# Storing only two of the three bf16 parts of q and k ahead of the loads for the row maxima

## The chip, the cores and the metric

The kernel runs on one core of a Trainium2 chip. The metric is the device time of one execution in microseconds (us), lower is better. The engines are TensorE (PE, its weight loads PEld), VectorE (DVE), ScalarE (ACT), GpSimd (POOL) and SyncE (SP), which here issues all DMAs.

## The reference

The input x has 16 images of 256 tokens and 128 channels. Four layers are added to it one after the other: x = x + layer(layernorm(x)). The first is a state-space layer with 32 heads. The second is a transformer block, the third mixes shifted tokens through gates, and the fourth is the same transformer block again. Only the attention inside the transformer block (it runs twice for each image, as "layer 0" and "layer 1" of the kernel) is touched:

```python
def _attention(src, Wq, bq, Wk, bk, Wv, bv, Wo, bo):
    q = (src @ Wq + bq).reshape(B, T, NHEAD, HEAD_DIM)      # 16 heads of 8
    k = (src @ Wk + bk).reshape(B, T, NHEAD, HEAD_DIM)
    v = (src @ Wv + bv).reshape(B, T, NHEAD, HEAD_DIM)
    scores = jnp.einsum('bqhd,bkhd->bhqk', q, k) * scale
    probs = jax.nn.softmax(scores, axis=-1)
    out = jnp.einsum('bhqk,bkhd->bqhd', probs, v).reshape(B, T, d)
    return out @ Wo + bo
```

It is followed by `x1 = ln(src + attn_out)`, a mixture of 8 experts and `ln(x1 + ff)`.

## The kernel before

The work is written as a list of "hops" (`PERIOD`), each with a name, a layer, a step and a lag. One pass over the list is a turn. In turn t a hop with lag l works on image t - l, so a turn holds pieces of up to six images, and there are 16 turns with a new image and some at either end in which the list is only partly filled (turns are counted from 0 here). Every engine walks through the same list in the same order and does its own part of each hop; semaphores connect the parts. An engine that waits in one hop delays all its later hops, so the order of the list is the schedule.

The score matrix is computed with bf16 operands. q and k (128 rows, one per head and channel, by 256 tokens) are each split into three bf16 parts that add up to the f32 value. The hop `q` does this, with step 1 for k and step 0 for q:

- PE multiplies (L746), ACT writes the f32 value `qkf` (L1034) and the first part (L1035).
- POOL subtracts the first part (L1494), casts the rest to the second part (L1496) and subtracts again for the third part (L1498), which raises `split_done`. Behind k's parts it also adds `b_o` to `src` (L1502) and `ln2_b` to `x` (L1503), for later hops.
- SP waits for `split_done` and stores the parts to DRAM in the layout in which they will be read: for q the first two parts, twice (L541); for k all three parts, three times (L545, L547).

The hop `mload` follows. SP waits until the stores of k and then of q have landed and loads both for the maxima (`k_max`, `q_max`, L556, four DMAs a side; only rows made of the first two parts are read). Behind them it stores what is left of q: the first two parts once more (L559) and the third part three times (L562). The hop `sload` loads all 72 rows (`k_stack`, `q_stack`, L571).

The hop `smax` multiplies `q_max` with `k_max` on PE (L765), and DVE takes the maxima (`rowmax`, L1295). They become one more row of `q_stack` (`maxt`), and the hops `es`, `exps` and `ep` do the scores, exponentials and the product with v.

In the list k comes first in layer 0 and q comes first in layer 1. The list around the changed hops:

```
layer 0: q0.1 down0.4 ... q0.0 ... experts0.2 ... mix1.0 ... tail1.3 ... mload0.0 tap0.6 xcopy0.2
         xcopy0.4 tap0.7 mix1.1 taps0.6 place0.0 tail1.4 taps0.7 mix1.2 bcp0.0 mix1.3 ... smax0.0
layer 1: q1.0 es0.1 exps0.1 own0.5 sum0.2 q1.1 up1.4 ... mload1.0 ... own0.6 ... sload1.0 ... smax1.0
```

Other work of POOL near these hops: the reciprocal roots of the layer norms (L1437 and L1439, for `experts0.2`, `mix1.0` and `tail1.3`), the addition of `mix_b` to x (`mix1.2`, L1513), `bc_prod` (`bcp0.0`, L1451), the sums of the mixing layer (L1519) and the products `own` (L1529). Other work of DVE there: the convolution taps (L1220, one input in PSUM, one in SBUF), the edge correction of the convolution (L1230, both inputs in SBUF, 6 columns), the normalisation of `mix1.1` (L1114), the last step of a layer norm (`tail1.4`, L1127, two instructions, both inputs in SBUF), the mixing products (L1408) and the decay products `att` (L1247).

Of the kernel before, what the change touches and what calls it, by code (L numbers as in the profile page):

```python
# [11 lines left out]
P = 128  # L12
BATCH, T, HID = 16, 256, 128
NT = T // P
# [181 lines left out]
def build(nc, d, out):  # L196
# [12 lines left out]
    with ctx:  # L209
# [3 lines left out]
        def sem(name):  # L213
            return ctx.enter_context(nc.semaphore(name))
# [155 lines left out]
        src_ready, split_done, nmax_ready = sem("src_ready"), [sem("q_split"), sem("k_split")], sem("nmax_ready")  # L370
        x1_ready, gate_in, gate_exp, we_ready = sem("x1_ready"), sem("gate_in"), sem("gate_exp"), sem("we_ready")
# [31 lines left out]
        for hop in hops:  # L403
            if (hop[0], hop[3]) in (("q", 1), ("mix", 2)):
                offsets[hop[:3]] = len(offsets) + 1

        bo_adds = {}
        for hop in hops:
            if (hop[0], hop[3]) == ("q", 1):
                bo_adds[hop[1], hop[2]] = len(bo_adds) + 1  # L410
# [90 lines left out]
        def _(e):  # L501
# [11 lines left out]
            for hop in hops:  # L513
# [20 lines left out]
                elif what == "q":  # L534
# [4 lines left out]
                    if k == 0:  # L539
                        for copy in range(2):  # L540
                            e.dma_start(dram(qk_scrd[0], 2 * copy * P * T, [[T, P], [P * T, 2], [1, T]]),  # L541
                                        qparts_b[0][:, 0:2, :]).then_inc(qk_stored[0], 16)
                    else:
                        for copy in range(2):
                            e.dma_start(dram(qk_scrd[1], copy * P * T, [[T, P], [2 * P * T, 3], [1, T]]),  # L545
                                        qparts_b[1][:, :, :]).then_inc(qk_stored[1], 16)
                        e.dma_start(dram(qk_scrd[1], 6 * P * T, [[T, P], [P * T, 3], [1, T]]),  # L547
                                    qparts_b[1][:, :, :]).then_inc(qk_stored[1], 16)
                elif what == "mload":
# [3 lines left out]
                    for side in (1, 0):  # L553
                        e.wait_ge(qk_stored[side], (96 * u + 32, 48 * (u + 1))[side])
                        for g in range(RG):
                            e.dma_start((q_max, k_max)[side][32 * g:32 * g + MAXROWS, :, :].rearrange("r s t -> r (s t)"),  # L556
                                        dram(qk_scrd[side], g * HPG * T, [[NH * T, MAXROWS], [1, HPG * T]])).then_inc(
                                            max_loaded[side], 16)
                    e.dma_start(dram(qk_scrd[0], 4 * P * T, [[T, P], [P * T, 2], [1, T]]),  # L559
                                qparts_b[0][:, 0:2, :]).then_inc(qk_stored[0], 16)  # L560
                    for copy in range(3):
                        e.dma_start(dram(qk_scrd[0], (6 + copy) * P * T, [[T, P], [1, T]]),  # L562
                                    qparts_b[0][:, 2, :]).then_inc(qk_stored[0], 16)
                elif what == "sload":
# [4 lines left out]
                    for side in (1, 0):  # L569
                        e.wait_ge(qk_stored[side], (96, 48)[side] * (u + 1))  # L570
# [335 lines left out]
        def _(e):  # L906
# [6 lines left out]
            for hop in hops:  # L913
# [114 lines left out]
                elif what == "q":  # L1028
                    t, b, u = bank(hop)
                    if nth[hop]:  # L1030
                        e.wait_ge(split_done[k], nth[hop])
                        e.wait_ge(qk_stored[k], (96, 48)[k] * nth[hop])
# [69 lines left out]
        def _(e):  # L1102
# [44 lines left out]
            for hop in hops:  # L1147
# [239 lines left out]
                elif what == "experts" and k == 3:  # L1387
                    ff, s = ff_b[lay], ln_slot(what, lay)
                    e.wait_ge(rstd_ready, roots["experts", lay, n, 2])
                    e.wait_ge(x_offset, offsets["q", lay, n])  # L1390
# [34 lines left out]
        def _(e):  # L1425
# [4 lines left out]
            for hop in hops:  # L1430
# [59 lines left out]
                elif what == "q":  # L1490
# [5 lines left out]
                    e.tensor_copy(qparts[:, 1, :], qr).then_inc(*own.step())  # L1496
                    e.wait_ge(*own.now())
                    e.tensor_tensor(qparts[:, 2, :], qr, qparts[:, 1, :], ALU.subtract).then_inc(split_done[k], 1)  # L1498
                    if k == 1:
                        e.wait_ge(rest_loaded, 16 * len(rest_consts))  # L1500
                        e.wait_ge(*full(("fn", lay, n, 1)))
                        e.tensor_tensor(src_b[lay][:, :, :], src_b[lay][:, :, :], bc(b_o[:, :], 1, NT), ALU.add).then_inc(src_bo, 1)  # L1502
                        e.tensor_tensor(xb[:, :, :], xb[:, :, :], bc(ln2_b[:, :], 1, NT), ALU.add).then_inc(x_offset, 1)  # L1503
# [78 lines left out]
```

## Time and profile before

| | |
|---|---|
| time, median of 3 runs | 2107.03 us (2103.94 to 2107.87) |
| the profiled execution | 2103.15 us, its span 2101.4 us |
| busy: PE, DVE, ACT, POOL | 91%, 83%, 71%, 37% of the span |
| mean granted TensorE clock | 0.966 of full speed |
| distance of two full turns | 119.4 us (the same DVE instruction at 1065.28 and at 1184.66 us) |

The span is the time from the first to the last instruction; 1.75 us of the execution lie outside it. In a full turn PE and DVE are busy almost all the time. At either end of the execution the list is only partly filled, and there the engines wait for single steps of the attention.

### The profile page before, as it was taken

To read this page: it belongs to the slowest core of one execution; us is meant where nothing else is said; L and a number is where in the kernel's file an instruction comes from. 1 tells how busy PE (TensorE), PEld (TensorE's weight loads), DVE (VectorE), ACT (ScalarE), POOL (GpSimd) and SP (SyncE) were. 2 spreads that over 40 slices of the span, in tenths; PEclk is the share of its full clock that TensorE was granted. 3 is DMA by queue.
4 is the path that set the end of the run, shared out by engine and by line. 5 is a ranking of instruction groups with operands and counts; after the bars stand their busy time and mean duration, and the time that the engine had idled before them with its cause. 6 is when DMAs were issued, how large, how long until landed. Compare 5 with 4: busy or idle time off the path is not lost.

```text
span 2101.4 us, 48245 instructions
## 1 busy us (share of the span) xinstructions
PE 1921.0 (91%) x16928; PEld 1491.0 (71%) x16928; DVE 1738.5 (83%) x4463; ACT 1488.0 (71%) x3207; POOL 775.6 (37%) x1139
## 2 busy tenths in 40 slices
PE   4779899999999999999999999999999999997757
PEld 3556677777877777786877778786777778774545
DVE  5776988989898988989898998989898898865643
ACT  4566768778686868778686877868686877855332
POOL 5313353525243343525244352424334352423120
PEclk8889999999999999999999999999999999998867
DMA  5021232211222222211222222121222221112110
GB/s 162 12 63 12 60 67 60 65 41 46 50 59 67 62 67 63 56 35 51 59 60 67 62 64 56 45 44 54 67 60 67 62 63 38 50 53 71 27 56 6
DMA packets 224576, 117.14 MB, mean 56 GB/s; under 512 B 124360, under 2 KB 210512, under 8 KB 219216
## 3 DMA queue, kind: packets, MB, share of 16 engines
q1 hardware_dynamic: 224336, 114.06, 21.5%
q8 instruction: 137, 2.24, 0.5%
q14 instruction: 103, 0.84, 0.1%
HBM read 67.60 MB, written 46.14 MB: 54 GB/s over the span
## 4 chain that ended last, share of the span: by engine, by line
PE 64%; DVE 23%; ACT 4%; issue 4%; SPq 2%; POOL 2%; DMA 1%; DVEq 0%; ACTq 0%; POOLq 0%
DVE nmax L1295 6%; PE psA L862 6%; PE psB L724 6%; DVE work L1220 5%; PE psB L874 5%; PE psA L874 5%; PE psA L699 5%; PE psB L803 3%; PE psB L862 3%; PE psA L630 3%; PE psB L699 2%; PE psA L803 2%; DVE att L1247 2%; DVE hid L1408 2%; PE psA L788 2%
## 5 line engine op out<-in xcount | busy, mean ns | idle before, releaser
L1247 DVE TENSOR_TENSOR att<-att,QK 128x1024 f32<-128x1024 f32 x192 | 251.2, 1341 | 15.2 <-ACT att L1003 15.1
L1529 POOL TENSOR_TENSOR own<-X,ccoef 128x512 f32<-128x512 f32 x128 | 160.2, 1257 | 206.7 <-PE psA L699 97.1
L1437 POOL TENSOR_SCALAR var_eps<-lnmv 128x2 f32<-128x2 f32 x128 | 40.4, 316 | 524.0 <-DVE lnmv L1110 521.3
L1220 DVE SCALAR_TENSOR_TENSOR work<-psA,c_conv_w,work 128x255 f32<-128x255 f32 (+2 forms) x450 | 195.4, 474 | 11.8 <-ACT work L961 11.8
L630 PE MATMUL psA<-xnT_a,c_w_in 128*128 128x256 f32 x608 | 177.9, 397 | 17.8 <-DVE hid L1220 8.7
L1072 ACT ACTIVATE hid<-psA,c_b 128x256 f32<-128x256 f32 x295 | 135.8, 485 | 79.4 <-PE psA L862 79.2
L1295 DVE TENSOR_REDUCE nmax<-psB 128x2 f32<-128x512 f32 x288 | 186.6, 680 | 1.1 <-PE psB L765 1.1
L862 PE MATMUL psA<-x1T,c_w 128*128 128x256 f32 x608 | 178.9, 394 | 1.5 <-DVE nmax L1295 1.3
L1049 ACT ACTIVATE pt<-psB 128x512 f32<-128x512 f32 x256 | 147.4, 614 | 31.5 <-PE psB L789 31.4
L1295 DVE TENSOR_REDUCE nmax<-psA 128x2 f32<-128x512 f32 x224 | 149.8, 681 | 15.1 <-PE psA L765 14.9
L1220 DVE SCALAR_TENSOR_TENSOR work<-psB,c_conv_w,work 128x255 f32<-128x255 f32 (+1 forms) x360 | 159.0, 474 | 2.7 <-ACT work L961 2.1
L874 PE MATMUL psB<-c_w,hid 128*128 128x128 f32 x1152 | 160.6, 285 | 0.4 <-ACT hid L1072 0.4
L874 PEld LDWEIGHTS psB<-c_w,hid 128*128 128x128 f32 x1152 | 148.3, 199 | 8.8 <-issue 4.2
L1519 POOL TENSOR_TENSOR O_sb<-O_sb,hid 128x256 f32<-128x256 f32 x128 | 98.8, 772 | 148.8 <-DVE hid L1408 141.6
L1049 ACT ACTIVATE pt<-psA 128x512 f32<-128x512 f32 x256 | 150.3, 618 | 0.1
L1379 DVE SCALAR_TENSOR_TENSOR ff<-psB,w_e,ff 128x128 f32<-128x128 f32 x288 | 86.8, 342 | 73.1 <-PE psB L874 71.4
L630 PE MATMUL psB<-xnT_a,c_w_in 128*128 128x256 f32 x480 | 137.9, 392 | 0.8 <-ACT hid L1072 0.7
L862 PE MATMUL psB<-x1T,c_w 128*128 128x256 f32 x416 | 125.3, 396 | 13.0 <-DVE nmax L1295 11.9
L630 PEld LDWEIGHTS psA<-xnT_a,c_w_in 128*128 128x128 f32 x608 | 107.3, 196 | 39.6 <-DVE hid L1220 10.3
L1003 ACT ACTIVATE att<-psA 128x512 f32<-128x512 f32 x176 | 96.6, 599 | 53.4 <-PE psA L670 51.9
L1003 ACT ACTIVATE att<-psB 128x512 f32<-128x512 f32 x208 | 114.9, 603 | 21.6 <-PE psB L670 18.8
L724 PE MATMUL psB<-c_w_out,Z 128*128 128x128 f32 x1024 | 124.3, 280 | 3.8 <-DVE c_w_out L1260 3.8
(326 smaller groups left out, 5375.3 us busy)
## 6 DMA issues: line engine op xcount, KB each, us to landing
qk_scr<-kparts SPq DMA_DIRECT2D x96, 192.0 KB, 2.4
k_stack<-qk_scr SPq DMA_DIRECT2D x32, 576.0 KB
q_stack<-qk_scr SPq DMA_DIRECT2D x32, 576.0 KB
qk_scr<-qparts SPq DMA_DIRECT2D x96, 128.0 KB, 1.9
k_max<-qk_scr SPq DMA_DIRECT2D x128, 64.0 KB, 2.0
q_max<-qk_scr SPq DMA_DIRECT2D x128, 64.0 KB, 2.0
lvl_scr<-work SPq DMA_DIRECT2D x32, 192.0 KB, 5.7
qk_scr<-qparts SPq DMA_DIRECT2D x96, 64.0 KB, 1.7
```

Of the source, the lines that this page charges most:

```text
L630: e.matmul(t[:, 0:T], w_in[:, first + j * P:first + (j + 1) * P], xnT_a[:, :], start=True, stop=True).then_inc(filled[b], 1)
L699: m = e.matmul(t[j * HD:(j + 1) * HD, f * P:(f + 1) * P], X[:, s, fc + j * HD:fc + (j + 1) * HD], att[:, 2 * f + j, :], start=False, stop= ...
L724: m = e.matmul(t[:, k * P:(k + 1) * P], Z[:, f, k * P:(k + 1) * P], w_out[:, f, :], start=(f == 0), stop=(f == NF - 1))
L862: e.matmul(t[:, 0:T], w_1[:, k, j * P:(j + 1) * P], x1T_b[lay][:, :], start=True, stop=True).then_inc(filled[b], 1)
L874: m = e.matmul(t[:, i * P:(i + 1) * P], hb[:, j, i * P:(i + 1) * P], w_2[:, 2 * k + j, :], start=(j == 0), stop=(j == 1))
L1003: e.activation(att[:, :, c:c + 64], t[:, :].rearrange("p (t h) -> p h t", h=HG), ACT.Exp).then_inc(drained[b], 1)
L1049: e.activation(pt_b[a % PTS][:, :, :].rearrange("p h q -> p (h q)"), t[:, :], ACT.Exp, scale=float(AD) ** -0.5).then_inc(drained[b], 1)
L1072: e.activation(hid_b[lay][k % 2][:, j, :], t[:, 0:T], ACT.Relu, bias=b_1[:, 2 * k + j:2 * k + j + 1]).then_inc(drained[b], 1)
L1220: m = e.scalar_tensor_tensor(out=cv[:, back:], in0=t[:, 0:T - back], scalar=conv_w[:, c, tap:tap + 1], in1=cv[:, back:], op0=ALU.mult, op1 ...
L1247: e.tensor_tensor(att[:, :, :], att[:, :, :], bc(QK[:, kq, :], 1, HG), ALU.mult).then_inc(att_done, 1)
L1295: e.tensor_reduce(nmax[:, i, p0:p0 + 2], t[:, :].rearrange("p (h k) -> p h k", k=T), AX.X, ALU.max).then_inc(drained[b], 1)
L1529: e.tensor_tensor(own_b[k % 2][:, :].rearrange("p (h c) -> p h c", c=HD), X[:, tt, h0 * HD:(h0 + HG) * HD].rearrange("p (h c) -> p h c", c ...
```

## The change

In hop `q` POOL makes only the second part and raises `split_done` behind it. SP stores only the first two parts, twice, for k as for q. The third parts move into hop `mload` on POOL: k's, then q's, each raising a new semaphore `third_done`, and behind them the two additions of `b_o` and `ln2_b`. In hop `mload` SP loads the side that was stored first first (layer 0 k, layer 1 q). Behind the loads it waits for k's third part, stores the rest of k in two DMAs and the first two parts of q once more, waits for q's third part and stores it three times with one DMA. DVE's later wait for `x_offset` is counted from the hop `mload`.

```diff
@@ SP, hop q
-                    if k == 0:
-                        for copy in range(2):
-                            e.dma_start(dram(qk_scrd[0], 2 * copy * P * T, [[T, P], [P * T, 2], [1, T]]),
-                                        qparts_b[0][:, 0:2, :]).then_inc(qk_stored[0], 16)
-                    else:
-                        for copy in range(2):
-                            e.dma_start(dram(qk_scrd[1], copy * P * T, [[T, P], [2 * P * T, 3], [1, T]]),
-                                        qparts_b[1][:, :, :]).then_inc(qk_stored[1], 16)
-                        e.dma_start(dram(qk_scrd[1], 6 * P * T, [[T, P], [P * T, 3], [1, T]]),
-                                    qparts_b[1][:, :, :]).then_inc(qk_stored[1], 16)
+                    for copy in range(2):
+                        first, step = ((2 * copy, 1), (copy, 2))[k]
+                        e.dma_start(dram(qk_scrd[k], first * P * T, [[T, P], [step * P * T, 2], [1, T]]),
+                                    qparts_b[k][:, 0:2, :]).then_inc(qk_stored[k], 16)
@@ SP, hop mload
-                    for side in (1, 0):
-                        e.wait_ge(qk_stored[side], (96 * u + 32, 48 * (u + 1))[side])
+                    for side in ((1, 0), (0, 1))[lay]:
+                        e.wait_ge(qk_stored[side], 64 * u + 32)
...
+                    e.wait_ge(third_done[1], u + 1)
+                    e.dma_start(dram(qk_scrd[1], 4 * P * T, [[T, P], [P * T, 2], [1, T]]),
+                                bc(qparts_b[1][:, 2, :], 1, 2)).then_inc(qk_stored[1], 16)
+                    e.dma_start(dram(qk_scrd[1], 6 * P * T, [[T, P], [P * T, 3], [1, T]]),
+                                qparts_b[1][:, :, :]).then_inc(qk_stored[1], 16)
                     e.dma_start(dram(qk_scrd[0], 4 * P * T, [[T, P], [P * T, 2], [1, T]]),
                                 qparts_b[0][:, 0:2, :]).then_inc(qk_stored[0], 16)
-                    for copy in range(3):
-                        e.dma_start(dram(qk_scrd[0], (6 + copy) * P * T, [[T, P], [1, T]]),
-                                    qparts_b[0][:, 2, :]).then_inc(qk_stored[0], 16)
+                    e.wait_ge(third_done[0], u + 1)
+                    e.dma_start(dram(qk_scrd[0], 6 * P * T, [[T, P], [P * T, 3], [1, T]]),
+                                bc(qparts_b[0][:, 2, :], 1, 3)).then_inc(qk_stored[0], 16)
@@ POOL, hop q, then hop mload
-                    e.tensor_copy(qparts[:, 1, :], qr).then_inc(*own.step())
-                    e.wait_ge(*own.now())
-                    e.tensor_tensor(qparts[:, 2, :], qr, qparts[:, 1, :], ALU.subtract).then_inc(split_done[k], 1)
-                    if k == 1:
-                        e.wait_ge(rest_loaded, 16 * len(rest_consts))
-                        e.wait_ge(*full(("fn", lay, n, 1)))
-                        e.tensor_tensor(src_b[lay][:, :, :], src_b[lay][:, :, :], bc(b_o[:, :], 1, NT), ALU.add).then_inc(src_bo, 1)
-                        e.tensor_tensor(xb[:, :, :], xb[:, :, :], bc(ln2_b[:, :], 1, NT), ALU.add).then_inc(x_offset, 1)
+                    e.tensor_copy(qparts[:, 1, :], qr).then_inc(split_done[k], 1)
+                elif what == "mload":
+                    for k in (1, 0):
+                        qr, qparts = qkf[:, k, :], qparts_b[k]
+                        e.wait_ge(split_done[k], nth[hop] + 1)
+                        e.tensor_tensor(qparts[:, 2, :], qr, qparts[:, 1, :], ALU.subtract).then_inc(third_done[k], 1)
+                    e.wait_ge(rest_loaded, 16 * len(rest_consts))
+                    e.wait_ge(*full(("fn", lay, n, 1)))
+                    e.tensor_tensor(src_b[lay][:, :, :], src_b[lay][:, :, :], bc(b_o[:, :], 1, NT), ALU.add).then_inc(src_bo, 1)
+                    e.tensor_tensor(xb[:, :, :], xb[:, :, :], bc(ln2_b[:, :], 1, NT), ALU.add).then_inc(x_offset, 1)
```

ACT's hop `q` now waits for `third_done` and for 64 instead of 96 and 48 counts of `qk_stored`, and `sload` waits for 64.

## Rows read from the trace of the kernel before

**Rows 1.** The page: busy time, share of the span and instructions of each engine

```profile
PE 1921.0 (91%) x16928; PEld 1491.0 (71%) x16928; DVE 1738.5 (83%) x4463; ACT 1488.0 (71%) x3207; POOL 775.6 (37%) x1139
```

**Rows 2.** Waits over the whole span: us in total, times, longest us

```profile
PEld psA L765 <- DMA q_max<-qk_scr: 14.5, 3, 9.4
```

**Rows 3.** Timeline, first image, layer 0: start us, us, engine, line, operation

```profile
132.15 0.48 ACT L1035 ACTIVATE qparts<-psA,c_bq 128x256 bf16<-128x256 f32 x1
...
133.61 0.67 POOL L1494 TENSOR_TENSOR qkf<-qkf,qparts 128x256 f32<-128x256 f32 x1
...
135.52 0.88 SPq L541 DMA_DIRECT2D qk_scr<-qparts  x2
...
143.81 0.28 PE L765 MATMUL psA<-k_max,q_max 32*128 32x256 bf16 x1 [3.13 <-DMA q_max<-qk_scr]
```

**Rows 4.** Timeline, last image but one, layer 1

```profile
1942.86 0.28 PE L765 MATMUL psA<-k_max,q_max 32*128 32x256 bf16 x1 [1.49 <-DMA q_max<-qk_scr]
```

**Rows 5.** Chain of work that ended last, last image, layer 1

```profile
2022.91 0.67 POOL qparts L1498
...
2024.76 0.68 POOL kparts L1498
...
2026.39 2.54 DMA qk_scr<-kparts
...
2032.14 1.97 DMA q_max<-qk_scr
```

**Rows 6.** Timeline, last image, layer 1

```profile
2028.99 1.71 SPq L556 DMA_DIRECT2D k_max<-qk_scr  x4
...
2034.15 0.39 PE L765 MATMUL psA<-k_max,q_max 32*128 32x256 bf16 x1 [9.00 <-DMA q_max<-qk_scr]
```

**Rows 7.** Timeline of POOL, a full turn, layer 0

```profile
1175.08 0.67 POOL L1498 TENSOR_TENSOR kparts<-qkf,kparts 128x256 bf16<-128x256 f32 x1
1175.72 0.72 POOL L1502 TENSOR_TENSOR src<-src,c_bo 128x256 f32<-128x256 f32 x1
1176.41 0.72 POOL L1503 TENSOR_TENSOR x<-x,c_ln_b 128x256 f32<-128x256 f32 x1
...
1185.30 0.73 POOL L1513 TENSOR_TENSOR x<-x,c_beta 128x256 f32<-128x256 f32 x1
```

**Rows 8.** Timeline of VectorE, the same turn

```profile
1187.26 0.17 DVE L1230 TENSOR_TENSOR work<-work,conv_edge 128x6 f32<-128x6 f32 x1
1187.37 0.61 DVE L1127 SCALAR_TENSOR_TENSOR x<-x,lnrs,c_ln_b 128x128 f32<-128x128 f32 x2
```

**Rows 9.** Chain of work that ended last, the same turn

```profile
1187.37 0.61 DVE x L1127 x2
```

**Rows 10.** Line 1127, from 1894.3 to 1896.5 us: ns min/median/max, first and last start

```profile
L1127 DVE SCALAR_TENSOR_TENSOR x<-x,lnrs,c_ln_b x2: 339/628/917, 1894.7 to 1895.5; 128x128 f32<-128x128 f32 x2
```

**Rows 11.** Timeline of POOL at that place

```profile
1894.70 0.72 POOL L1513 TENSOR_TENSOR x<-x,c_beta 128x256 f32<-128x256 f32 x1
```

**Rows 12.** Timeline of POOL and VectorE, layer 1 of a full turn

```profile
1115.50 1.34 POOL L1502 TENSOR_TENSOR src<-src,c_bo 128x256 f32<-128x256 f32 x1
...
1116.29 0.63 DVE L1194 TENSOR_TENSOR work<-SPL,c_neg_a 128x64 f32<-128x64 f32 x1
...
1117.49 1.49 POOL L1529 TENSOR_TENSOR own<-X,ccoef 128x512 f32<-128x512 f32 x1
...
1120.90 3.22 DVE L1247 TENSOR_TENSOR att<-att,QK 128x1024 f32<-128x1024 f32 x2
```

**Rows 13.** Timeline of VectorE, the turn in which a tap ended late

```profile
1423.91 2.50 DVE L1220 SCALAR_TENSOR_TENSOR work<-psB,c_conv_w,work 128x255 f32<-128x255 f32 x6
1426.87 0.17 DVE L1230 TENSOR_TENSOR work<-work,conv_edge 128x6 f32<-128x6 f32 x1 [0.46 <-DVE work L1220]
...
1543.60 2.49 DVE L1220 SCALAR_TENSOR_TENSOR work<-psB,c_conv_w,work 128x255 f32<-128x255 f32 x6
```

**Rows 14.** Timeline of VectorE, first image in the mixing layer

```profile
235.43 0.61 DVE L1114 SCALAR_TENSOR_TENSOR src<-x,lnmv,lnrs 128x128 f32<-128x128 f32 x2 [1.21 <-POOL lnrs L1439]
```

More of the change, by code:

```diff
@@ L370, in build @@
         src_ready, split_done, nmax_ready = sem("src_ready"), [sem("q_split"), sem("k_split")], sem("nmax_ready")
+        third_done = [sem("q_third"), sem("k_third")]
         x1_ready, gate_in, gate_exp, we_ready = sem("x1_ready"), sem("gate_in"), sem("gate_exp"), sem("we_ready")
@@ L403, in build @@
         for hop in hops:
-            if (hop[0], hop[3]) in (("q", 1), ("mix", 2)):
+            if (hop[0], hop[3]) in (("mload", 0), ("mix", 2)):
                 offsets[hop[:3]] = len(offsets) + 1
@@ L408, in build @@
         for hop in hops:
-            if (hop[0], hop[3]) == ("q", 1):
+            if hop[0] == "mload":
                 bo_adds[hop[1], hop[2]] = len(bo_adds) + 1
@@ L569, in _ @@
                     for side in (1, 0):
-                        e.wait_ge(qk_stored[side], (96, 48)[side] * (u + 1))
+                        e.wait_ge(qk_stored[side], 64 * (u + 1))
                         e.dma_start((q_stack, k_stack)[side][0:ROW_MAX, :, :].rearrange("r s t -> r (s t)"),
@@ L1030, in _ @@
                     if nth[hop]:
-                        e.wait_ge(split_done[k], nth[hop])
-                        e.wait_ge(qk_stored[k], (96, 48)[k] * nth[hop])
+                        e.wait_ge(third_done[k], nth[hop])
+                        e.wait_ge(qk_stored[k], 64 * nth[hop])
                     e.wait_ge(filled[b], u + 1)
@@ L1389, in _ @@
                     e.wait_ge(rstd_ready, roots["experts", lay, n, 2])
-                    e.wait_ge(x_offset, offsets["q", lay, n])
+                    e.wait_ge(x_offset, offsets["mload", lay, n])
                     e.wait_ge(*own.now())
```

## Prediction

> **What bounds the kernel.** I read the page first [rows 1]: TensorE is busy 91% of the span and VectorE 83%, and in a full turn both are near their limit. So a step of the attention's preparation costs time only where one of them stands still for it. The list of waits shows where that is [rows 2]: over 32 attentions TensorE waits for the maxima's loads only three times, 14.5 us in all on the weight-load side, 9.4 of them once. In all other attentions the loads have long landed and earlier hops of the list set the start of `smax`. The timelines give the three places: the first image in layer 0 [rows 3], the last image but one in layer 1 [rows 4] and the last image in layer 1 [rows 5, 6]. On TensorE's own side these waits are 3.13, 1.49 and 9.00 us. The chain of work passes through them, POOL's split, the store, its landing, the loads [rows 5].
>
> In the full turns I then looked for what POOL's work touches, because that work is moved. The chain of work goes there through VectorE, instruction after instruction, and one of its pieces is `tail1.4`, L1127 [rows 8, 9].
>
> **What the change gives, place by place.**
>
> First image, layer 0. ACT's first part of q is there at 132.63, but POOL begins q's remainder only at 133.61, since k's third part and the two additions are ahead of it [rows 3]. Without these it could begin up to 0.98 us earlier; I take 0.84, with a little for the hand-over from ACT. q's own third part, 0.67 us (the duration in [rows 5, 7]), leaves the way of the stores too. The stores, the loads and their landing follow in the same order, so `smax` comes 1.5 us earlier than 143.81. TensorE's wait of 3.13 us leaves room for it. **-1.5 us.**
>
> Last image but one, layer 1. The loads gain one third part, 0.67 us, and the landing of k's third store; the order q before k also lets q's loads run while k's stores land. That is over 3 us by the sum of the next paragraph, but TensorE waits only 1.49 [rows 4]. **-1.5 us.**
>
> Last image, layer 1. k's remainder can start where q's third part starts now, 2022.91, and k's parts are ready after a subtraction and a cast, at 2024.1, where now they end at 2025.44 [rows 5]. Now the third store leaves at 2026.39 and takes 2.54 us to land, and the eight loads run from 2028.99 on, k's four in 1.71 us and q's four in about as long again, the last of them issued at 2032.14 [rows 5, 6]. After the change the two k stores leave at 2024.1 and 2024.5 and land by 2027.05 at the same 2.54. q's stores left at 2022.9 and 2023.3, so q's loads run from 2025.3 to 2027.1 in that shadow. k's run from 2027.1 to 2028.9, the last is issued at 2028.5 and lands 1.97 us later [rows 5]. TensorE starts at 2030.5 instead of 2034.15. **-3.6 us.** Its wait shrinks from 9.00 to about 5.4, so all of it is taken out of the wait.
>
> Together -6.6 us. All other stores and loads have slack. Issues fall from nine to eight an attention at the same bytes; SP's new waits for the third parts stand behind the maxima's loads, and what is queued behind them, `lvl` and `sload`, is needed by hops many microseconds later. I cost both at nothing. If that slack were gone, a late third part would delay `es`, and TensorE with it.
>
> **What the move on POOL costs.** In layer 0 of a full turn the third parts and the additions leave a place where POOL was otherwise idle: k's third part and both additions run from 1175.08 to 1177.13 there, all at their shortest durations [rows 7], beside taps that read one input from PSUM. They go to the hop `mload`, just ahead of `mix1.2`, which now begins at 1185.30 [rows 7]. By the spacings of [rows 7] (0.64, then 0.69) the four take 0.64 + 0.64 + 0.69 + 0.69 = 2.66 us: k's third from 1185.30, q's from 1185.94, `b_o` 1186.58 to 1187.30, `ln2_b` 1187.27 to 1187.99, and then `mix1.2` and `bcp0.0` behind them without a gap until about 1189.4. POOL was idle there from 1186.7 on. Now VectorE has L1230 at 1187.26 and the pair L1127 from 1187.37 to 1187.98 [rows 8].
>
> Such a pair does not run beside a POOL instruction. At 1894.65 an instruction of L1127 takes 917 ns and the other 339 [rows 10]; POOL's addition runs from 1894.70 to 1895.42 [rows 11], and the long one ends 0.15 us after it. So it waited for POOL's end although it had started first. In layer 1 L1194, 64 columns, takes 0.63 us and ends 0.08 after POOL's addition; that addition took 1.34 instead of 0.72, so POOL waits as well [rows 7, 12]. The Trainium skill, "SBUF — State Buffer", section "Who interferes with whom", has the rule: a VectorE instruction with two SBUF inputs and a GpSimd instruction that reads SBUF exclude each other, and whoever issues first keeps the port for the whole instruction. The trace agrees on the exclusion and not on the order, since the 917 ns instruction had the earlier start; applied to the order of starts worked out here, the rule would give the same result as the rows.
>
> Worked through: L1230 slips in at 1187.30 between two additions, as L1194 did. The first L1127 waits for the end of `ln2_b` at 1187.99 and ends at 1188.14. `mix1.2` had to wait, runs the 0.60 us that a blocked addition takes after its release (1.34 - 0.74 in [rows 12]), and ends at 1188.74. The second L1127 ends 0.15 later, 1188.89, against 1187.98 now: **+0.91 us**. It's a piece of the chain [rows 9], and the taps behind it follow at once, so the turn grows by it. How much comes through is shown once: at 1426.87 L1230 started 0.36 us late [rows 13], and that turn lasted 119.69 us (1423.91 to 1543.60) where its neighbours last 119.39, 0.30 more. I take 0.06 off: +0.85 us. The bounds per turn: 0.57 if only one POOL instruction is met (917 - 346), 1.5 if L1230 misses its gap and each of three instructions waits. I take the value of the exact alignment.
>
> It repeats in the turns that have `taps0.6`, `tail1.4` and `mload0.0`: 13 of them, turns 4 to 16, in all of which the present timeline is the same within 0.1 us. **13 x 0.85 = +11.0 us.** In turn 3 the same place holds L1114, whose pair starts 0.03 us before POOL is free for k's third part [rows 14]: **+0.9 us** by the same reckoning, between 0 and 1.2.
>
> Layer 1 of a full turn: q's third part leaves a place where it only ran ahead of a wait of POOL for TensorE, and comes behind k's. `own` at 1117.49 [rows 12] starts some 1.1 us later, alone (about 1.04 us), and ends near 1119.7, before the two `att` at 1120.90. Cost 0. Without that margin of 1.2 us the cost would be up to 0.8 in each of 16 turns, which is what one `own` adds to the pair of `att` today (3.22 against 2 x 1.21).
>
> **Sum.** -6.6 + 11.0 + 0.9 = +5.3 us. The profiled execution, 2103.15, becomes 2108.4. It lies 3.9 us under the median of the runs; the difference is carried over, so the median 2107.03 becomes **2112.3 us**.
>
> **Rivals.**
> 1. *The exclusion costs nothing*, because POOL's block falls between VectorE's two-input instructions or the slip is made up in the turn. For it: the moved work took nothing from VectorE in its old place, and POOL has 63% idle. Against it: the block is 4 us without a gap around a fixed chain of VectorE. Then the three places at the ends are all: 2107.03 - 6.6 = 2100.4, faster. It decides from where less than 0.5 us of collisions a turn is left (6.6 over 14 turns).
> 2. *Half of it*: one collision a turn, 0.5 us, 13 times, +0.5 in turn 3: -6.6 + 7.0 = +0.4, 2107.4, no difference.
> 3. *Every collision at its worst*: 14 x 1.45 - 6.6 = +13.7, 2120.7. It decides from L1230 missing its gap, a matter of 0.1 us.
> 4. *The change doesn't do what it says*: the ends keep their waits because the store of k lands later in two parts than in three. Nothing in [rows 5] speaks for it; with the collisions it gives 2107.03 + 11.9 = 2118.9.
>
> **Chances.** The forecast (collisions of 0.85 to 1.1 a turn, 2111 to 2116 with the scatter of the runs) 0.48, rival 3 0.07, rival 4 0.05, rival 2 0.25, rival 1 0.15. The measurement can tell about 0.2%, 4.2 us, from no change. Faster by more 0.15; within it 0.25; slower 0.60. The range leaves out rival 1 and a little of rival 3: 2104 to 2120. The forecast's own range is 2109 to 2117.
>
> **What the new profile would show.** The waits for the maxima's loads: 3.13 becomes about 1.6, 1.49 goes, 9.00 becomes about 5.4. SP's third k store is gone ahead of `mload`. In turns 4 to 16 L1127 of `tail1.4` has a duration near 0.8 to 1.0 us instead of 0.35, POOL is busy from the third parts to `bc_prod` without a gap, and two full turns are 120.2 us apart instead of 119.4. If L1127 stays at 0.35, or the turns stay at 119.4, the prediction is wrong and the kernel is faster. If L1230 takes 0.8 too, the time is nearer to 2120. If `att` grows in layer 1, I placed `own` wrongly.

## The result and the profile after

The changed kernel takes 2127.09 us, the median of 4 runs (2124.05 to 2128.53), beside 2105.49 us for the kernel before on the same chip (2103.29 to 2107.87). The ratio is 1.0099, with a 95% interval of 1.0087 to 1.0112: slower by 21.6 us. I predicted 2112.3 us, between 2104 and 2120. The sign was right, but the forecast change was +5.3 us where +21.6 was measured, and the time lies outside the range.

The profiled execution took 2128.53 us with a span of 2126.7. The profiled one of before took 2103.15, so the two traces differ by 25.4 us, 4 us more than the medians.

The page of the changed kernel, where [rows 1] stood, shows TensorE with the same instructions and 17 us more of busy time:

```profile
PE 1938.3 (91%) x16928; PEld 1503.5 (71%) x16928; DVE 1754.9 (83%) x4463; ACT 1494.4 (70%) x3207; POOL 768.6 (36%) x1139
```

Its list of waits over the whole span, two rows:

```profile
PEld psA L834 <- issue: 20.9, 15, 3.6
...
PE psA L834 <- DVE x L1127: 18.4, 14, 3.4
```

The same two rows before:

```profile
PEld psA L834 <- issue: 3.6, 1, 3.6
PE psA L834 <- DVE x L1127: 3.4, 1, 3.4
```

L834 is TensorE's transpose of the `x` that L1127 writes. The one wait of 3.4 us, in the last image, was there before; the 13 of the full turns are new. Timelines of a full turn in layer 0, POOL, then VectorE, then TensorE. They answer to [rows 7, 8], one turn earlier:

```profile
1079.46 0.67 POOL L1501 TENSOR_TENSOR kparts<-qkf,kparts 128x256 bf16<-128x256 f32 x1
...
1081.41 0.72 POOL L1505 TENSOR_TENSOR x<-x,c_ln_b 128x256 f32<-128x256 f32 x1
1082.09 0.72 POOL L1515 TENSOR_TENSOR x<-x,c_beta 128x256 f32<-128x256 f32 x1
1082.77 0.77 POOL L1451 TENSOR_TENSOR bc_prod<-work 128x256 f32<-128x256 f32 x1
```

```profile
1081.42 0.73 DVE L1230 TENSOR_TENSOR work<-work,conv_edge 128x6 f32<-128x6 f32 x1
1082.07 1.62 DVE L1127 SCALAR_TENSOR_TENSOR x<-x,lnrs,c_ln_b 128x128 f32<-128x128 f32 x2
```

```profile
1083.84 0.30 PE L834 MATMUL psA<-c_ident,x 128*128 128x128 f32 x1 [1.17 <-DVE x L1127]
```

Read the ends. L1230 starts at 1081.42, 0.01 us behind the start of the addition of `ln2_b`, and ends at 1082.15, 0.02 behind its end. The first L1127 starts at 1082.07 and ends behind `mix1.2` (1082.81); the second ends at 1083.69, behind `bc_prod` (1083.54). So each of VectorE's three instructions waits out one POOL instruction. POOL's own keep 0.72 us, and only `bc_prod` has 0.05 more. Matched one by one with those of the trace before, the three add 0.57, 0.52 and 0.47 us of delay: 1.55 together. The two L1127 do this in all 13 full turns; L1230 takes 0.73 to 0.75 us in 11 of them and 0.25 and 0.38 in the other two (turns 12 and 13).

That is not all of it. The turns are not equally long. ScalarE's `maxT`, one of its two in each of three turns in a row (timeline of ScalarE, changed kernel; the other one of each turn is left out):

```profile
499.43 0.36 ACT L1041 ACTIVATE maxT<-psA 16x256 bf16<-16x256 bf16 x1
...
621.89 0.36 ACT L1041 ACTIVATE maxT<-psA 16x256 bf16<-16x256 bf16 x1
...
742.74 0.36 ACT L1041 ACTIVATE maxT<-psA 16x256 bf16<-16x256 bf16 x1
```

One turn lasts 122.46 us and the next 120.85, where 119.39 was the rule before. The table by stretches, for two stretches of about the same length that begin with L834, one in a long and one in a short turn (columns: us, then the busy time of TensorE, its weight loads, VectorE, ScalarE and POOL, the granted clock, DMA share, GB/s), and TensorE's timeline in the long one:

```profile
596.10:600.20 4.10, 4.10 (x13) 3.34 (x14) 3.74 (x10) 1.77 (x5) 0.73 (x1) 0.58 0.72 187
1083.80:1088.00 4.20, 4.17 (x32) 3.76 (x32) 3.98 (x10) 2.38 (x7) 0.73 (x1) 1.00 0.69 191
```

```profile
596.10 0.30 PE L834 MATMUL psA<-c_ident,x 128*128 128x128 f32 x1 [1.18 <-DVE x L1127]
...
597.16 1.06 PE L893 MATMUL psA<-srcT,c_w_mix 128*128 128x256 f32 x2
```

In 4.1 us TensorE starts 13 matmuls of the long turn, and in 4.2 us 32 of the short one. Behind the wait for L1127 the granted clock is 0.58 in the mean, most of the stretch at 1.2 GHz. Two matmuls of L893 take 1.06 us where they take 0.59 at the full clock. In the trace of before the clock is never low between 300 and 1890 us; in that of the changed kernel it is low in eight places in that time. Each begins at L834, between 0.7 us ahead of its start, inside the wait, and 0.3 us behind it.

The wait of [rows 4] is gone. The other two ends of the execution, timelines of TensorE in the first image and, with SP, in the last, which answer to [rows 3, 6]:

```profile
144.22 0.28 PE L765 MATMUL psA<-k_max,q_max 32*128 32x256 bf16 x1 [2.34 <-DMA q_max<-qk_scr]
```

```profile
2059.48 0.37 PE L765 MATMUL psA<-k_max,q_max 32*128 32x256 bf16 x1 [5.43 <-issue]
```

```profile
2054.20 1.71 SPq L551 DMA_DIRECT2D q_max<-qk_scr  x4
2055.96 1.81 SPq L551 DMA_DIRECT2D k_max<-qk_scr  x4
```

In the last image k's loads now come last, so it fits that TensorE's wait there no longer carries the name of q's.

The account of the two traces, from `maxT` of each attention in both (the changed kernel's start less that of before). Up to the third attention it is 0.6 us late; the traces of the experiments lie there between 3.7 us early and 1.7 late. The 13 turns 4 to 16 cost 1.46 us each, 19.0. The eight half clocks cost 12.4, in seven of those turns seen as 1.2 to 2.8 us more than 1.46. Two odd losses of before, 1.3 us near 432 and 0.3 at [rows 13], are not there any more: -1.6. The turn behind them adds 0.6. The last image but one gives back 1.55 and the last 4.07. Together 0.6 + 19.0 + 12.4 - 1.6 + 0.6 - 1.55 - 4.07 = 25.4 us.

The odd loss near 432 is a late landing, TensorE's timeline before:

```profile
429.72 0.27 PE L788 MATMUL psB<-q_stack,k_stack 96*128 96x256 bf16 x1 [1.19 <-DMA q_stack<-maxT]
```

Waits of 0.7 to 1.2 us for this load are in single turns of some of the traces below, here or at other places, and in none of the changed kernel's full turns. They are scatter between executions, up to about 1.3 us each.

### The profile page after: what moved, and what is told of

Its sections match the earlier page's. It is cut to its first block, busy times and chain, and to the rows that moved or that the text cites. A ratio compares the mean times of both kernels' runs of the same rounds, so it can differ in the third digit from the quotient of the medians.

```text
span 2126.7 us, 48213 instructions
## 1 busy us (share of the span) xinstructions
PE 1938.3 (91%) x16928; PEld 1503.5 (71%) x16928; DVE 1754.9 (83%) x4463; ACT 1494.4 (70%) x3207; POOL 768.6 (36%) x1139
## 4 chain that ended last, share of the span: by engine, by line
PE 66%; DVE 21%; ACT 4%; issue 4%; SPq 2%; POOL 1%; DMA 1%; DVEq 0%; ACTq 0%; POOLq 0%
DVE nmax L1295 6%; PE psA L862 6%; PE psB L724 6%; PE psB L874 5%; PE psA L874 5%; PE psA L699 5%; DVE work L1220 4%; PE psB L862 3%; PE psB L803 3%; PE psA L630 3%; PE psB L699 3%; PE psA L803 2%; PE psA L788 2%; DVE att L1247 2%; PE psB L630 2%
## 5 line engine op out<-in xcount | busy, mean ns | idle before, releaser
L1531 POOL TENSOR_TENSOR own<-X,ccoef 128x512 f32<-128x512 f32 x128 | 154.1, 1209 | 212.8 <-PE psA L699 112.3
L1003 ACT ACTIVATE att<-psB 128x512 f32<-128x512 f32 x208 | 114.9, 603 | 21.6 <-PE psB L670 18.8
```

What stands on the lines that cost most here:

```text
L1003: e.activation(att[:, :, c:c + 64], t[:, :].rearrange("p (t h) -> p h t", h=HG), ACT.Exp).then_inc(drained[b], 1)
L1531: e.tensor_tensor(own_b[k % 2][:, :].rearrange("p (h c) -> p h c", c=HD), X[:, tt, h0 * HD:(h0 + HG) * HD].rearrange("p (h c) -> p h c", c ...
```

## The experiments

Three ideas were tested: that POOL's block costs by colliding with VectorE, that TensorE's wait costs a second time through its clock, and against both, that SP's later stores and new waits cost. Ratios are to the kernel before, run beside them on the same chip.

**e1_layer0_back.** Layer 0's POOL work out of `mload`, to the end of hop `q`:

```diff
-                elif what == "mload":
+                if (what, lay, k) == ("q", 0, 0) or (what, lay) == ("mload", 1):
                     for k in (1, 0):
...
```

The counts of `x_offset` and `src_bo` follow. What was expected:

> The changed kernel, with layer 0's third parts and its two additions taken out of the hop mload again and put behind q's split, at the end of the hop q; the stores, the loads and all of layer 1 stay as changed. My theory: all that the full turns lost (two full turns 120.9 to 122.4 us apart instead of 119.4) comes from POOL's block meeting VectorE's L1230 and L1127. Then the full turns are back at 119.4 us, L1230 and L1127 at 0.17 and 0.35 us, TensorE is granted the full clock through all full turns, and only the gains at the ends are left: 1.5 and 4 us in the last two images and 0.8 in the first, so some 6 us under the kernel before, about 2100 us. Rival: SP's side costs the time (k's third stores behind the maxima's loads, the later landing of the last store, the new waits in SP's queue): then the full turns stay longer and the time stays near 2120 to 2127 us.

Measured: 2122.26 us, ratio 1.0076 (1.0064 to 1.0089). Neither theory had this. L1230 and L1127 are short again, as I expected, but the turns last 120.8 us. The timeline of VectorE, then that of POOL, show why:

```profile
1189.37 1.35 DVE L1122 SCALAR_TENSOR_TENSOR ff<-ff,lnmv,c_ln_g 128x128 f32<-128x128 f32 x2
...
1192.33 0.61 DVE L1127 SCALAR_TENSOR_TENSOR x<-ff,lnrs,x 128x128 f32<-128x128 f32 x2 [0.88 <-POOL lnrs L1439]
```

```profile
1190.53 0.78 POOL L1505 TENSOR_TENSOR x<-x,c_ln_b 128x256 f32<-128x256 f32 x1
1191.28 0.22 POOL L1437 TENSOR_SCALAR var_eps<-lnmv 128x2 f32<-128x2 f32 x1
```

The block now stands ahead of a root of the experts' norm. The pair L1122, 0.61 us before, waits out two POOL instructions, and POOL comes to the root at 1191.28, so VectorE then waits 0.88 for it. That is 1.4 us a turn by another route. TensorE waits 0.37 us ahead of L834 in most of these turns, and one of them has a half clock. The expectation failed in taking q's end for empty: in the kernel before, q's third part ends just ahead of that pair. One place was replaced by another bad one; the SP theory is tested by e8 below.

**e2_adds_back.** Only the two additions back into `q`, behind k's split; the third parts stay in `mload`:

```diff
+                if what == "mload":
                     for k in (1, 0):
...
+                if (what, lay, k) == ("q", 0, 1) or (what, lay) == ("mload", 1):
                     e.wait_ge(rest_loaded, 16 * len(rest_consts))
...
```

> The changed kernel, with only layer 0's two additions (b_o, ln2_b) put back into the hop q of side k; the two third parts stay in mload. POOL's block ahead of mix1.2 is then 2 instructions (1.28 us) longer than before instead of 4 (2.66 us). Theory that each of VectorE's three instructions (L1230, L1127 twice) waits for the end of the POOL instruction under way and POOL for none of them: bc_prod now runs from about 1187.3 to 1188.0 by the times of the kernel before, so L1230 waits 0.55 us and the pair after it finds POOL idle: +0.5 to 0.6 us a turn, 7 us over 13 turns, less 6 at the ends: about 2107 us, and TensorE's wait ahead of L834 is too short (0.2 us) to cost it the clock. The working of my prediction (L1230 slips into a gap, a POOL instruction waits too) gives about 0.3 to 0.5 us a turn and 2104 us. Rival that the sheer lateness of the third parts or of SP's stores counts: no gain against the changed kernel.

Measured: 2101.63 us, ratio 0.9981 (0.9972 to 0.999). VectorE and POOL in a full turn:

```profile
1187.92 0.72 DVE L1230 TENSOR_TENSOR work<-work,conv_edge 128x6 f32<-128x6 f32 x1
1188.56 0.60 DVE L1127 SCALAR_TENSOR_TENSOR x<-x,lnrs,c_ln_b 128x128 f32<-128x128 f32 x2
```

```profile
1187.90 0.72 POOL L1451 TENSOR_TENSOR bc_prod<-work 128x256 f32<-128x256 f32 x1
```

L1230 starts 0.02 us behind `bc_prod` and waits all of it out; the pair finds POOL idle. The three end 0.55 us later, of which 0.43 shows in the length of the turn. The theory of one POOL instruction for each of VectorE's gives the two rows. The time is 5 us under its 2107: 0.43 for 0.55 explains 1.6 us of that, and the odd loss near 432, which this trace doesn't have, another 1.3.

**e3_four_idle_adds.** The kernel before, with four POOL additions that nothing reads:

```diff
+        dum_b = [sb("dum", [P, T], BF16)] * 4
...
+                elif (what, lay) == ("mload", 0):
+                    e.wait_ge(rest_loaded, 16 * len(rest_consts))
+                    for d_ in dum_b:
+                        e.wait_ge(*own.now())
+                        e.tensor_tensor(d_[:, :].rearrange("p (i c) -> p i c", i=NT), bc(mix_b[:, :], 1, NT),
+                                        bc(ln2_b[:, :], 1, NT), ALU.add).then_inc(*own.step())
```

> The kernel before, with nothing moved, and four POOL additions of 128x256 on constants into a tile that nothing reads, in the hop mload of layer 0 (2.7 to 3 us of POOL, where the changed kernel has the third parts and the additions). Theory of the collisions: the same loss in the full turns as in the changed kernel, 1.5 us a turn in 13 turns, and TensorE's half clock behind it in about eight of them (1.4 us each), and none of the gains at the ends: 26 to 32 us above the kernel before, 2132 to 2138 us. Rival that the third parts' lateness or SP's order is what costs: under 5 us above the kernel before.

Measured: 2118.07 us, ratio 1.0061 (1.0043 to 1.008), so 12 us, under half of what I expected and far over the rival's 5. VectorE (its lines are one higher here):

```profile
1195.31 0.40 DVE L1231 TENSOR_TENSOR work<-work,conv_edge 128x6 f32<-128x6 f32 x1
1195.64 1.07 DVE L1128 SCALAR_TENSOR_TENSOR x<-x,lnrs,c_ln_b 128x128 f32<-128x128 f32 x2
```

Only two of the three wait, L1231 for 0.23 us and the second L1128 for 0.47: the four additions wait for each other, 3.21 us for the four, so VectorE meets them at other moments. A turn without a half clock costs 0.55 us more. TensorE waits 0.3 us ahead of its transpose of `x` (0.97 in one turn), and there are four half clocks in the full turns, each worth about 1.5 us; one is in the turn with the wait of 0.97. POOL work that no one needs, with SP's queue as before, thus costs as much as that; how much depends on where VectorE's instructions meet it.

**e4_busy_tensor_engine.** The changed kernel, TensorE's transposes of `place` done three times:

```diff
-                    for i in range(NT):
+                    for i in list(range(NT)) * 3:
                         for hg in range(H // HG):
```

> The changed kernel, with the eight transposes of place (L620) done three times, the same data into the same bank, so that TensorE works for about 1 us of the 1.17 us in which it now waits for L1127. If its half clock in some of the full turns (matmuls of L893 at twice their time from 596.1 to 600.2 us) comes from that wait, then the half clock goes from all full turns, all of them are 120.9 us long, and the time falls by 8 to 11 us against the changed kernel, to about 2117 us. Rival: the half clock has another cause (the rest of the chip, or chance); then it stays in as many turns, and the time is 2127 us.

Measured: 2114.92 us, ratio 1.0045 (1.0032 to 1.0057), 12 us under the changed kernel although TensorE does 0.9 us more in every turn. Timeline of TensorE:

```profile
1072.91 1.50 PE L620 MATMUL psA<-ident_bf,s_wide 128*128 128x128 bf16 x24
1074.69 0.30 PE L834 MATMUL psA<-c_ident,x 128*128 128x128 f32 x1 [0.28 <-DVE x L1127]
...
1075.37 0.60 PE L893 MATMUL psA<-srcT,c_w_mix 128*128 128x256 f32 x2
```

The wait is 0.28 us instead of 1.17, no full turn has a half clock, and a typical one is 1.43 us longer than before. From `maxT` of the third attention to that of the 30th this trace loses 17.7 us on the one before, the changed kernel's 30.4: the difference of 12.7 us is that of the half clocks, 12.4 in the account. (This trace is also 4.3 us ahead at the third attention, for which see e13.) TensorE's standing still ahead of L834 costs the clock, then.

**e5_eight_memsets.** The kernel before, with POOL instructions that write but read nothing:

```diff
+        dum_b = [sb("dum", [P, T], BF16)] * 8
...
+                    for d_ in dum_b:
+                        e.wait_ge(*own.now())
+                        e.memset(d_[:, :], 0.0).then_inc(*own.step())
```

> The kernel before with eight memsets of a tile that nothing reads, in the hop mload of layer 0: about as long on POOL as the four additions of e3_four_idle_adds (eight times 0.3 to 0.35 us), but they read nothing from SBUF. If VectorE's instructions wait for POOL's reading of SBUF, L1230 and L1127 keep 0.17 and 0.35 us while the memsets run, and at most mix1.2 and bc_prod behind them, up to 3 us later than before, meet something else: within 4 us of the kernel before. Rival: they wait for any POOL instruction that uses SBUF, or for POOL's order: then L1230 and L1127 are longer by what is left of a memset (0.1 to 0.3 us each), 5 to 10 us in all, and half clocks of TensorE may add to it.

Measured: 2105.5 us, ratio 0.9996 (0.9987 to 1.0005). POOL, then VectorE:

```profile
1185.48 2.89 POOL L1509 MEMSET dum<- 128x256 bf16 x8
1188.33 0.73 POOL L1519 TENSOR_TENSOR x<-x,c_beta 128x256 f32<-128x256 f32 x1
```

```profile
1187.46 0.17 DVE L1231 TENSOR_TENSOR work<-work,conv_edge 128x6 f32<-128x6 f32 x1
1187.57 0.61 DVE L1128 SCALAR_TENSOR_TENSOR x<-x,lnrs,c_ln_b 128x128 f32<-128x128 f32 x2
```

All three run at their shortest durations in the middle of the memsets, and `mix1.2` and `bc_prod` come 3 us later than before at no cost. POOL being busy, and POOL being late, are both free here. What costs is a POOL instruction that reads SBUF beside a VectorE instruction with two SBUF inputs. By the Trainium skill, "SBUF — State Buffer", section "Who interferes with whom", such a VectorE instruction contends with a GpSimd instruction that reads SBUF and "not with one that only writes it"; this run agrees.

**e8_best_of_both.** Layer 0's POOL work in the order of before, all else as changed:

```diff
                     e.tensor_copy(qparts[:, 1, :], qr).then_inc(split_done[k], 1)
+                    if lay == 0:
+                        e.wait_ge(split_done[k], nth[hop] + 1)
+                        e.tensor_tensor(qparts[:, 2, :], qr, qparts[:, 1, :], ALU.subtract).then_inc(third_done[k], 1)
+                if (what, lay) == ("mload", 1):
                     for k in (1, 0):
...
+                if (what, lay, k) == ("q", 0, 1) or (what, lay) == ("mload", 1):
                     e.wait_ge(rest_loaded, 16 * len(rest_consts))
...
```

> The changed kernel, with all of POOL's work in layer 0 in the order of the kernel before: each third part right behind its split, the two additions behind k's third part. SP's stores and loads and all of layer 1 stay as changed. My theory, after the run with all four behind q's split cost 1.4 us in each full turn at L1122, is that any place counts only by what of VectorE it meets, and that the old place meets nothing. Then the full turns are back at 119.4 us with L1230, L1127 and L1122 at their short durations, and the gains in the last two images stay (1.5 and 3 to 4 us): 5 to 6 us under the kernel before, 2099 to 2101 us, and 1.5 to 4 us under the run with only the additions put back. Rival: SP's third stores behind the loads cost something in each full turn; then it is no faster than the kernel before.

Measured: 2097.52 us, ratio 0.9953 (0.9941 to 0.9966): 8.7 us faster than before, more than the 5 to 6 I had from the ends. The two profiled executions differ by 5.6: 4.3 in the last two images and 1.3 for the odd loss near 432. The other 3 us of the medians are not explained. Its trace has the full turns at 119.4 us and no half clock in them. SP's part of the change costs nothing in full turns, so that rival falls.

**e9_old_load_order.** The same with `for side in (1, 0)`, k's loads first in both layers.

> The kernel of e8_best_of_both with the maxima's loads in the old order, k's side first, in both layers. In the last image k is stored last, so q's four loads (1.7 us of issuing) then stand behind k's instead of ahead of them. Theory: the gain of the last image (about 4 us between the last two attentions' maxima) falls to 2 to 2.5 us, that of the last image but one (1.5 us, all of TensorE's wait) stays, and nothing changes elsewhere: 1.5 to 2 us more than e8_best_of_both. Rival: the earlier stores alone give the gain, and the order is worth nothing.

Measured: 2099.37 us, ratio 0.9962 (0.9948 to 0.9975). TensorE in the last image:

```profile
2030.27 0.39 PE L765 MATMUL psA<-k_max,q_max 32*128 32x256 bf16 x1 [7.44 <-DMA q_max<-qk_scr]
```

The wait was 9.00 before, is 7.44 here and 5.49 in e8. Not all of the last difference is the order of the loads. The chain of work in the last image has, ahead of the first load, this store in e9 and then this one in e8:

```profile
2022.03 2.92 DMA qk_scr<-kparts
```

```profile
2021.28 1.97 DMA qk_scr<-qparts
```

k's second store took 2.92 us to land here, where each of the four stores of e8 took 1.9 to 2.0. Landings as late as that occur with the new order too: the same wait is 6.76 us in e1, 6.96 in e4 and 7.14 in e13, and 5.3 to 5.5 in the other runs. Without the late landing this one would be 0.9 us shorter, which leaves, as an estimate, 1.0 us for the order of the loads and 2.5 for the earlier stores. The times of e8 and e9 differ by 1.9 us, with intervals that overlap, so the order is worth something between 1.0 and 1.9.

**e10_three_moved** and **e11_one_moved.** Three POOL instructions in layer 0's `mload` (both third parts and `ln2_b`), and one (`ln2_b`). The edit of e10 against the changed kernel; e11 is e8 with its last two lines:

```diff
+                if (what, lay, k) == ("q", 0, 1) or (what, lay) == ("mload", 1):
...
                     e.tensor_tensor(src_b[lay][:, :, :], src_b[lay][:, :, :], bc(b_o[:, :], 1, NT), ALU.add).then_inc(src_bo, 1)
+                if what == "mload":
                     e.tensor_tensor(xb[:, :, :], xb[:, :, :], bc(ln2_b[:, :], 1, NT), ALU.add).then_inc(x_offset, 1)
```

> The changed kernel with only b_o's addition put back in layer 0, so three POOL instructions (1.97 us) are ahead of mix1.2 instead of four or, in e2_adds_back, two. The staircase theory, each of VectorE's three instructions waits for one POOL instruction: L1230 0.73 us, the first L1127 0.89, the second 0.35, so two full turns are about 1.0 us longer than 119.4 (two instructions moved: 0.43 measured; four: 1.5), 13 us in all less 6 at the ends, 2112 us, plus 1.4 for each half clock, if TensorE's wait of about 0.7 us is enough for one. Rival, a cost in proportion to POOL's time: nearly the same per turn, but spread over all three instructions.

> The kernel of e8_best_of_both with one POOL instruction in layer 0's mload, the addition of ln2_b. The foot of the staircase (two moved 0.43 us a full turn, three 0.98, four 1.5): bc_prod then ends at about 1187.35 us by the times of the kernel before, 0.1 us behind the start of L1230, so L1230 takes at most 0.1 to 0.2 us longer and the pair of L1127 nothing: under 0.15 us a turn, within 2 us of e8_best_of_both. Rival, a cost in proportion to POOL's time moved: 0.3 us a turn, 4 to 5 us.

Measured: 2116.16 us for three, ratio 1.0045 (1.0029 to 1.006), and 2095.53 for one, ratio 0.9959 (0.9943 to 0.9975). With three, VectorE:

```profile
1196.20 0.73 DVE L1230 TENSOR_TENSOR work<-work,conv_edge 128x6 f32<-128x6 f32 x1
1196.86 1.15 DVE L1127 SCALAR_TENSOR_TENSOR x<-x,lnrs,c_ln_b 128x128 f32<-128x128 f32 x2
```

and with one:

```profile
1186.97 0.17 DVE L1230 TENSOR_TENSOR work<-work,conv_edge 128x6 f32<-128x6 f32 x1
1187.07 0.61 DVE L1127 SCALAR_TENSOR_TENSOR x<-x,lnrs,c_ln_b 128x128 f32<-128x128 f32 x2
```

This is a staircase and no slope. One POOL instruction more costs a turn nothing (POOL's block ends 0.13 us behind L1230's start in that trace, and it isn't held up), two 0.43 us, three 0.98, four 1.46: each further one catches one more of VectorE's. With three, TensorE's wait of 0.70 us ahead of L834 is followed by a half clock in six of the full turns, each worth about 1.5 us.

**e12_filler_everywhere** and **e13_filler_first_image.** e8 with e4's threefold transposes, in all images, and in the first alone.

> The control of e4_busy_tensor_engine: the same threefold transposes of place in the kernel of e8_best_of_both, in which TensorE doesn't wait for L1127 in the full turns. If the filler gives nothing by itself, it now costs up to its 1.0 us in each of 13 full turns, less what TensorE has of slack behind it, and may save some us in the first image, where it shortened the half clock: 0 to 13 us above e8_best_of_both. Rival: the filler helps by itself, then it is faster than e8_best_of_both, and the 12 us of e4_busy_tensor_engine weren't the price of the half clock in the full turns.

> The kernel of e8_best_of_both with the threefold transposes in the first image alone, where TensorE waits for the maxima's loads anyway. In e4_busy_tensor_engine the half clock from 154.7 us was 3.4 us long instead of 10.2 and the second attention came 2 to 3 us earlier. Theory: the same here, 2 to 4 us less than e8_best_of_both, 2094 to 2096 us. Rival: it was chance in the first image's loads; no difference.

Measured: 2107.66 us, ratio 1.0015 (1.0005 to 1.0024), and 2098.97 us, ratio 0.9966 (0.9954 to 0.9978). Where TensorE doesn't wait, the filler costs 0.83 us in a typical turn of the trace, 10 us by the medians and 13 by the ratios, since e8 ran on another chip; so the 12 us that it gains in the changed kernel are no gain of its own. Each of the two traces has two of the odd waits for `q_stack`, 1.1 to 1.2 us. In the first image alone the filler gives nothing that these runs show; the earlier second attention in the one trace of e4 was chance or came from that kernel's other timing. That stays open.

## Why the prediction was right in sign and wrong in size

**First image, -1.5.** Half right. TensorE's wait fell from 3.13 to 2.34 us, 0.8. q's remainder waits for ACT now, as worked out, and from the end of ACT's first part to q's first store it is 1.25 us instead of 2.89, but k's four loads took SP 2.49 us to issue instead of 1.69, a cost that I had at nothing.

**Last image but one, -1.5.** Right: the wait is gone, 1.55 us between the attentions' `maxT`.

**Last image, -3.6.** Right: the wait was to become 5.4 and is 5.43. e9 shows that the stores and the order of the loads both have a part in it. There was some luck in the 0.03, since late landings make this wait 1.3 to 1.7 us longer in three of the other runs. The 4.07 of the account has another 0.5 us; e8, with about the same wait, has only 2.79 there, and the cause of this scatter stays open.

**SP's waits and late stores, 0.** Right by e8.

**Layer 1's window, 0.** Right: the pair `att` takes 3.22 us as in [rows 12], and the turns of e8, which keep the change there, are as long as before.

**Turn 3, +0.9.** The collision was as large as said: the two L1114 end 0.92 us later in all. How much of it stayed can't be told from the scatter of the first images.

**The collisions, 13 x 0.85 = 11.0.** This is the step that failed, and it was mis-sized in two ways.

First, the size of the collision: 1.55 us of late ends and 1.46 us of turn, where I took 0.91 and 0.85. "L1230 slips in at 1187.30 between two additions" was wrong in 11 of the 13 turns. L1230 starts 0.02 us ahead of the end of the addition of `b_o`, which is too late: it waits out the next one and gets in at that one's end. Where it starts 0.23 us ahead, in turn 12, it does get in and takes 0.25 us. So such a place exists, and at its 0.04 us ahead (1187.26 and 1187.30) the prediction took L1230 for in time. "`mix1.2` had to wait" was wrong too: it took 0.72 us, and the two L1127 waited for it and for `bc_prod`. I had taken POOL's 1.34 us of [rows 12] over to a place where POOL doesn't wait. (The 0.74 that I subtracted there is in none of the rows shown; it is about the time to the end of L1192, shown further down.) The thirteen turns weren't all alike before either, as I had said: [rows 13] is one of them, with L1230 0.36 us late. All this was my rival 3, with a bound of 1.5 and a chance of 0.07. With 13 x 1.46 + 0.9 and my ends it gives 13 us, 2120. The exact alignment that I trusted hung on 0.04 us; a step that decides between 0.85 and 1.5 on so little should not have been settled by them, and rival 3 deserved far more than 0.07.

Second, a term that the sum didn't have. I let the turn grow by VectorE's delay and never asked what TensorE does meanwhile. Its L834 waits 1.17 us for the late `x`, and at that wait the granted clock falls to 1.2 GHz in eight places, 12.4 us in the profiled execution. I had put this at nothing, without a reason. e4 removes them with the collisions left in place; e12 is its control. With both corrected the sum is 0.9 + 19.0 + 12.4 - 6.6 = 25.7 us, beside the 25.4 of the traces. The medians bear out a somewhat smaller sum, since the profiled execution was the slowest of its four.

The rule of the Trainium skill named in the prediction fits the measurement only in part. It has the exclusion and the waiting for a whole instruction, both seen here. The order of issue can't be read from the start times. The first L1127 starts at 1082.07, 0.02 us ahead of `mix1.2`, and yet `mix1.2` keeps its 0.72 us and L1127 waits; at [rows 10, 11] L1127 is 0.05 ahead and waits too. Whether it asked for the memory later than it started, these traces don't show.

## What to carry to other kernels

Work that is moved on an engine with 63% idle costs by what it lands beside. List the instructions of the other engine that exclude it in the new place, and count one whole instruction of wait for each of them that meets the block. Then follow the delay to TensorE: a new wait of 0.3 to 1.2 us there, close behind another one, cost 1.2 to 2.8 us more through the clock in some of the turns. When a change mixes a good part with a bad one, separate them: here the early stores and the load order with POOL's old order in layer 0 run in 2097.5 us, 8.7 under the kernel before and 29.6 under the change.

## What the runs showed of the hardware that I had not expected

In these places the exclusion goes one way: VectorE waited 0.47 to 0.57 us and POOL's instructions kept 0.72 to 0.77. In layer 1 both get longer ([rows 12]). There VectorE's L1192, with both inputs in SBUF, comes first (timeline of VectorE before):

```profile
1115.44 0.81 DVE L1192 TENSOR_TENSOR SPL<-SPL,work 128x640 f32<-128x640 f32 x1
```

It starts 0.06 us ahead of POOL's addition of 1115.50, which then takes 1.34 us and so ends 0.59 behind L1192's end; L1194 in its turn ends 0.08 behind the addition. So POOL does wait where VectorE gets in first. L1192 had started 0.09 us ahead of the end of POOL's instruction before. In layer 0 the starts 0.02 us (L1230) and 0.06 us (the first L1127) ahead of an end came too late. L1230's start 0.23 us ahead, in turn 12, was in time (timelines of VectorE and POOL, changed kernel):

```profile
1326.67 0.25 DVE L1230 TENSOR_TENSOR work<-work,conv_edge 128x6 f32<-128x6 f32 x1
```

```profile
1326.17 0.73 POOL L1504 TENSOR_TENSOR src<-src,c_bo 128x256 f32<-128x256 f32 x1
```

What decides between these, and whether it is the same for all instructions, isn't shown.

The half clock doesn't come in every turn, and not at every wait. In the 13 full turns it came eight times at a wait of 1.17 us ahead of L834, six at 0.70 (e10), once at 0.37 (e1), four times in e3 (three at 0.3, one at 0.97), and never at 0.15 (e2) or without a wait there (before, e5, e8, e9, e11, e12, e13). e4 has 0.28 us and none: there TensorE works 0.9 us longer just ahead of the wait than in e3. And one wait alone didn't do it. In a full turn before, TensorE waits longer than that shortly ahead:

```profile
1187.39 0.67 PE L888 MATMUL psA<-srcT,c_w_val 128*128 128x256 f32 x2 [1.41 <-ACT srcT L1077]
```

This wait of 1.3 to 1.4 us is in all these turns, in every run, and with no second one behind it the clock stayed full. In the changed kernel the second follows 1.1 us of work later. What picks the turn isn't settled by these runs.

POOL's memsets, eight in 2.89 us, took nothing from VectorE.
